# Combining a mixture of experts: weights built during the experts' stage, results kept by slot, row-tiled products in the combine

## The reference, cut to what matters

```python
cap = int(EXPERT_CAPACITY * T / E)                       # 2 * 256 / 8 = 64
scores = jnp.einsum('BTC,CE->BTE', x, gate_w)
probs = jax.nn.softmax(scores, axis=-1)
top_p, top_idx = jax.lax.top_k(jnp.transpose(probs, (0, 2, 1)), cap)
xin = jnp.take_along_axis(x[:, None, :, :], top_idx[..., None], axis=2)
h = jax.nn.gelu(jnp.einsum('BElC,ECH->BElH', xin, w1), approximate=False)
y = jnp.einsum('BElH,EHC->BElC', h, w2)
y = y * top_p[..., None]
out = jnp.zeros((B, T, C), x.dtype).at[b_idx, top_idx].add(y)
...
x = x + gb * out
```

## Time and profile before

| | us |
|---|---|
| median of 3 runs | 1366.04 (1364.01 to 1376.72) |
| the profiled execution | 1369.83 |
| its span, first to last instruction | 1368.0 |
| mean granted TensorE clock in the span | 0.882 of full |

### The profile page before, as it was taken

How to read it: one execution, slowest core, us unless ns; L and a number is a source line. 1 busy time by engine, 2 the same in 40 slices (tenths; PEclk the granted TensorE clock), 3 DMA queues, 4 the chain that set the end, 5 groups by cost and what they waited for, 6 DMA issues and landing times. The chain is left out here.

```text
span 1368.0 us, 23917 instructions
## 1 busy us (share of the span) xinstructions
PE 1073.3 (78%) x6664; PEld 818.5 (60%) x6665; DVE 870.2 (64%) x1675; ACT 693.1 (51%) x1535; POOL 637.9 (47%) x938
## 2 busy tenths in 40 slices
PE   1999966899787799889998889973463399999950
PEld 1577742344386588778888788862242267777640
DVE  2477647201187599999999999992466633433327
ACT  1455432343244688888888888860242233433320
POOL 2000002100021689999999999980000556666630
PEclk9898857999999799999999999995555599999985
DMA  6000000111100200000000000003210011111135
GB/s 194 1 1 1 1 1 0 34 43 33 44 0 22 64 13 13 12 12 12 23 12 12 12 12 16 19 1 129 71 31 23 6 35 43 42 42 42 41 75 167
DMA packets 48617, 46.23 MB, mean 34 GB/s; under 512 B 4857, under 2 KB 44482, under 8 KB 48210
## 3 DMA queue, kind: packets, MB, share of 16 engines
q1 hardware_dynamic: 39474, 28.71, 7.3%
q0 software_dynamic: 4608, 9.45, 2.5%
q10 hardware_dynamic: 4496, 7.60, 1.6%
HBM read 36.74 MB, written 9.01 MB: 33 GB/s over the span
## 5 line engine op out<-in xcount | busy, mean ns | idle before, releaser
L1220 DVE TENSOR_TENSOR_SCAN s_hs<-s_dA,bank 128x1024 f32<-128x1024 f32 x128 | 291.5, 2277 | 11.2 <-PE bank L1617 10.5
L1477 POOL TENSOR_SCALAR s_dbuT<-s_dtuT,s_BT 128x256 f32<-128x256 f32 x512 | 242.3, 503 | 11.3 <-POOL s_bc L1415 5.4
L1338 ACT ACTIVATE s_dA<-s_dt,aneg 128x255 f32<-128x255 f32 x512 | 211.8, 495 | 0.2
L1617 PE MATMUL bank<-const,s_dbuT 128*128 128x128 f32 x1024 | 136.3, 277 | 3.1 <-POOL s_dbuT L1477 3.1
L1231 DVE TENSOR_TENSOR s_hc<-s_hs,bank 128x1024 f32<-128x1024 f32 (+1 forms) x128 | 130.2, 1017 | 5.0 <-PE bank L1644 1.6
L2142 PE MATMUL bank<-w,x_xT 128*128 x288 | 127.2, 565 | 5.4 <-issue 3.9
L1635 PE MATMUL bank<-const,s_hc 128*128 128x128 f32 x832 | 114.3, 276 | 21.1 <-DVE s_hc L1231 21.1
L1617 PEld LDWEIGHTS bank<-const,s_dbuT 128*128 128x128 f32 x1024 | 116.8, 143 | 6.5 <-POOL s_dbuT L1477 4.0
L1635 PEld LDWEIGHTS bank<-const,s_hc 128*128 128x128 f32 x832 | 95.7, 142 | 24.9 <-DVE s_hc L1231 24.9
L2180 ACT ACTIVATE x_a<-bank 128x448 f32<-128x448 f32 x72 | 39.2, 545 | 140.2 <-PE bank L2142 140.2
L2102 POOL DMA_INDIRECT x_xg<-hf_rows,x_src x72 | 69.8, 969 | 72.3 <-DVE x_src L2200 42.4
(11 more groups left out here) (303 smaller groups left out, 2332.1 us busy)
## 6 DMA issues: line engine op xcount, KB each, us to landing
s_Crow<-C_rows SPq DMA_DIRECT2D x48, 128.0 KB, 2.9
w<-in_w SPq DMA_DIRECT2D x16, 256.0 KB, 3.0
o_yr<-y_rows SPq DMA_DIRECT2D x8, 512.0 KB, 3.9
w<-in_w ACTq DMA_DIRECT2D x1, 3584.0 KB, 13.2
x_res<-in_x SPq DMA_DIRECT2D x4, 512.0 KB
gate<-gates_d SPq DMA_DIRECT2D x2, 1024.0 KB, 5.8
s_gate<-gates_d SPq DMA_DIRECT2D x2, 1024.0 KB, 7.4
hf_rows<-r_rows SPq DMA_DIRECT2D x8, 256.0 KB, 2.2
```

Source lines behind the costliest of these rows:

```text
L1220: dve.tensor_tensor_scan(flat(hs[:, j % 2]), flat(dA[:, j % RING]), bDbu[j % 2], 0.0, ALU.mult, ALU.add).then_inc(S["scanned"], 1)
L1338: ins = act.activation(dA[:, j % RING, h, n, 1:], dt[:, k, h, 1:], ACT.Exp, scale=m.aneg[:, h, 2 * j + n:2 * j + n + 1])
L1477: ins = pool.tensor_scalar(dbuT[:, j % RING, c, n, :], dtuT[:, k, c, :], BT[:, k, c, 2 * j + n:2 * j + n + 1], 1.0, ALU.mult, ALU.mult)
L1617: mm = pe.transpose(out[:, h, n, c * P:(c + 1) * P], dbuT[:, j % RING, c, n, h * P:(h + 1) * P], ident)
```

## The change

In five places:

- **Constants.** One column more: C_SLOT holds 1 + (partition mod 64).
- **Attention and combine.** The making of `m.spread` moves from POOL's start in attention to POOL in the combine, for its memory is used in between.
- **Route.** ACT copies the turned probabilities out (`chance`), SP stores them to device memory (`m.prob_d`, 128 KB). DVE makes the slot list a second time in bfloat16 (`listed16`), and SP stores it too (`m.place_d`, 64 KB).
- **Experts.** After the weights of each expert, SP spreads rows of `m.place_d` and `m.prob_d` over partitions: for the pair of sequences with the expert's number, each sequence's row of 2,048 entries (8 experts x 256 tokens) goes to 64 partitions, first sequence to the lower and second to the upper half. DVE then makes all the weights of that pair with one instruction, `(place == slot) * prob`, into `m.pickT`. The second product has its operands swapped: `g` is the weights' side and `w2` the moving side, 16 products of 128 columns per half in place of 4 of 512. Its result has the slot in the partition.
- **Combine.** No one-hots, transposes or copies are left. For each pair, half of the tokens and expert, two products over 64 rows each, one on the lower and one on the upper half of the array, into two different banks; then DVE's two products with the gate and one add. The loop is written out; four pairs have banks of their own. The gate load stays at the head, but now only DVE's first product waits for it.

Memory is laid out anew (`m.pickT` shares memory with `m.xin`, `m.taps` with `m.yT`).

```diff
@@ route_phase
-            tick(dve.tensor_copy(left[:], ps[0][:, 0:L]))
-            settle()
+            dve.tensor_copy(left[:], ps[0][:, 0:L]).then_inc(s_copied, 1)
+            dve.wait_ge(s_copied, 1)
...
             dve.tensor_tensor(listed[:], place[:], taken[:], ALU.mult).then_inc(s_out, 1)
+            dve.tensor_tensor(listed16[:], place[:], taken[:], ALU.mult).then_inc(s_list16, 1)
...
+        @block.scalar
+        def _(act):
+            act.wait_ge(s_copied, 1)
+            act.activation(chance[:], ps[0][:, 0:L], ACT.Copy).then_inc(s_chance, 1)
+
+        @block.sync
+        def _(sp):
+            rows = lambda t: t.rearrange("b (e t) -> (b e) t", e=E0)
+            sp.wait_ge(s_chance, 1)
+            sp.dma_start(rows(m.prob_d), chance[:]).then_inc(s_kept, 16)
+            sp.wait_ge(s_list16, 1)
+            sp.dma_start(rows(m.place_d), listed16[:]).then_inc(s_kept, 16)
+            sp.wait_ge(s_kept, 32)
@@ expert_phase, sync (after the two weight loads of an expert)
+                    sp.wait_ge(chosen[k], r + 1)
+                    for j in range(2):
+                        row = bass.ds(4 * r + 2 * k + j, 1)
+                        part = slice(CAP * j, CAP * (j + 1))
+                        for dst, src in ((place[k], m.place_d), (prob[k], m.prob_d)):
+                            sp.dma_start(dst[part, :], src[row, :].rearrange("o n -> (o n)").partition_broadcast(CAP))\
+                              .then_inc(spread[k], 16)
@@ expert_phase, tensor
                         for h in range(HC0):
                             pe.wait_ge(gelued[h], 4 * r + 2 * k + a + 2)
-                            mm = pe.matmul(ps[4 + a][:, :], w2[:, k, h, :], g[:, a, h, :], start=(h == 0),
-                                           stop=(h == HC0 - 1))
+                        for j in range(N // P):
+                            for h in range(HC0):
+                                mm = pe.matmul(ps[4 + a][:, j * D:(j + 1) * D], g[:, a, h, j * P:(j + 1) * P],
+                                               w2[:, k, h, :], start=(h == 0), stop=(h == HC0 - 1))
                         mm.then_inc(result[k][a], 1)
@@ expert_phase, vector (after the two copies to m.yT)
+                    dve.wait_ge(spread[k], 64 * (r + 1))
+                    dve.scalar_tensor_tensor(m.pickT[:, bass.ds(2 * r + k, 1), :].rearrange("p o n -> p (o n)"), place[k],
+                                             m.const[:, C_SLOT:C_SLOT + 1], prob[k], ALU.is_equal, ALU.mult)\
+                       .then_inc(chosen[k], 1)
@@ combine_phase (all of its old body goes)
         @block.sync
         def _(sp):
             sp.dma_start(gate[:], gate_rows(m, GB0)).then_inc(s_gate, 16)
             sp.wait_ge(s_gate, 16)
 
+        @block.gpsimd
+        def _(pool):
+            pool.tensor_copy(m.spread[:], m.const[:, C_REP + NST:C_REP + 2 * NST].unsqueeze(2).broadcast_to(
+                [P, NST, P])).then_inc(s_spread, 1)
+            pool.wait_ge(s_spread, 1)
+            pool.memset(m.spread[32:64], 0.0).then_inc(s_spread, 1)
+            pool.wait_ge(s_spread, 2)
+
         @block.tensor
         def _(pe):
...
+            for p in range(PAIRS):
+                if p >= 4:
+                    pe.wait_ge(s_read, 2 * (p - 3))
+                for c in range(NCH):
+                    for e in range(E0):
+                        for k in range(2):
+                            rows = slice(CAP * k, CAP * (k + 1))
+                            t = e * L + c * P
+                            mm = pe.matmul(ps[2 * (p % 4) + k][:, c * D:(c + 1) * D], m.pickT[rows, p, t:t + P],
+                                           m.yT[rows, e, p * D:(p + 1) * D], start=(e == 0), stop=(e == E0 - 1))
+                mm.then_inc(s_out, 1)
+
+        @block.vector
+        def _(dve):
+            dve.wait_ge(s_gate, 16)
+            for p in range(PAIRS):
+                dve.wait_ge(s_out, p + 1)
+                if p >= 2:
+                    dve.wait_ge(s_sum, p - 1)
+                for k in range(2):
+                    dve.tensor_tensor(out[:, p % 2, 2 * k:2 * k + 2, :],
+                                      ps[2 * (p % 4) + k][:, 0:L].rearrange("p (c d) -> p c d", c=NCH),
+                                      gate[:, 2 * p + k:2 * p + k + 1, :].broadcast_to([P, NCH, D]), ALU.mult)\
+                       .then_inc(s_read, 1)
+                dve.wait_ge(s_read, 2 * p + 2)
+                xs = m.x_res[:, 2 * NCH * p:2 * NCH * (p + 1), :]
+                dve.tensor_tensor(xs, out[:, p % 2], xs, ALU.add).then_inc(s_sum, 1)
+            dve.wait_ge(s_sum, PAIRS)
@@ build, before gather_phase
+                    whole = sb("xin", [P, 5 * E0 * L + E0 * B * CAP])
+                    m.xin = whole[:, 5 * E0 * L:].rearrange("p (e n) -> p e n", e=E0)
+                    m.pickT = whole[:, 0:PAIRS * E0 * L].rearrange("p (r n) -> p r n", r=PAIRS)
```

More of the change, by code:

```diff
@@ L493, in _ @@
                     .then_inc(S["w_own"], 1)
[L494 to L498, removed]
             pool.wait_ge(S["w_prep"], 1)
             pool.tensor_scalar(m.aneg[:], m.aneg[:], -1.0, 1.0, ALU.mult, ALU.mult).then_inc(S["w_own"], 1)
-            pool.wait_ge(S["w_own"], NH + 4)
+            pool.wait_ge(S["w_own"], NH + 2)
             def body(n0, n1, n2, n3, n4, odd):
@@ L778, in route_phase @@
         listed = sb("listed", [P, L])
+        listed16 = sb("listed16", [P, L], BF16)
+        chance = sb("chance", [P, L])
         s_in, s_own, s_out, s_back = sem("rt_in"), sem("rt_own"), sem("rt_out"), sem("rt_back")
+        s_copied, s_chance, s_list16, s_kept = sem("rt_copied"), sem("rt_chance"), sem("rt_list16"), sem("rt_kept")
         ident = m.const[:, C_ID:C_ID + P]
@@ L894, in expert_phase @@
         g = sb("g", [P, 2, HC0, N])
+        place1 = sb("place1", [P, E0 * L], BF16)
+        place = [m.spread[:].rearrange("p n q -> p (n q)"), place1[:]]
+        prob = [m.xn2[:, TILES // 2 * k:TILES // 2 * (k + 1), :].rearrange("p t d -> p (t d)") for k in range(2)]
+        spread = [sem(f"e_spread{k}") for k in range(2)]
+        chosen = [sem(f"e_chosen{k}") for k in range(2)]
         loaded = [sem(f"e_loaded{k}") for k in range(2)]
@@ L903, in _ @@
         def _(pool):
-            for free in (*result[0], *result[1], *gelued, *kept):
+            for free in (*result[0], *result[1], *gelued, *kept, *chosen):
                 pool.sem_inc(free, 1)
@@ L972, in combine_phase @@
-        s_gate, s_out, s_sum = (sem("c_" + n) for n in ("gate", "out_ps", "sum"))
-        ident = m.const[:, C_ID:C_ID + P]
-        iota = m.const[:, C_IOTA:C_IOTA + CAP]
-        block = ctx.enter_context(nc.Block())
[L978 to L1015, removed]
-                        if b is not None:
-                            dve.wait_ge(S["pickT_ps"][k], a)
-                        lists(a, k)
-                if b is not None:
-                    for k in range(2):
-                        dve.wait_ge(s_out, 2 * b + k + 1)
-                        dve.wait_ge(s_sum, 2 * b + 2)
-                        dve.tensor_tensor(out[:, k], ps[6 + k][:, 0:L].rearrange("p (c d) -> p c d", c=NCH),
-                                          gate[:, bass.ds(2 * b + k, 1), :].broadcast_to([P, NCH, D]),
-                                          ALU.mult).then_inc(S["prod"][k], 1)
-                    for k in range(2):
-                        dve.wait_ge(S["prod"][k], b + 2)
-                        xs = m.x_res[:, bass.ds(b * 2 * NCH + k * NCH, NCH), :]
-                        dve.tensor_tensor(xs, out[:, k], xs, ALU.add).then_inc(s_sum, 1)
-            dve.wait_ge(s_gate, 16)
-            rounds(dve, body)
@@ L1034, in _ @@
+        gate = sb("gate2", [P, B, D])
+        out = sb("moe0", [P, 2, 2 * NCH, D])
+        s_gate, s_out, s_read, s_sum, s_spread = (sem("c_" + n) for n in ("gate", "out_ps", "read", "sum", "spread"))
+        block = ctx.enter_context(nc.Block())
         @block.sync
@@ L1069, in _ @@
-            rounds(pe, body)
-        @block.scalar
-        def _(act):
-            def body(a, b):
-                if a is not None:
-                    for k in range(2):
-                        act.wait_ge(S["pickT_ps"][k], a + 1)
-                        for q in range(2):
-                            act.activation(pickT[:, k, 2 * q:2 * q + 2, :],
-                                           ps[2 * k + q][:, :].rearrange("p (a t) -> p a t", a=2),
-                                           ACT.Copy).then_inc(S["pickT"][k], 1)
-                    for k in range(2):
-                        act.wait_ge(S["y_ps"][k], a + 1)
-                        act.activation(ysl[:, k], ps[4 + k][:, :].rearrange("p (a d) -> p a d", d=D), ACT.Copy)\
-                           .then_inc(S["ysl"][k], 1)
-            rounds(act, body)
+            for p in range(PAIRS):
[9 more added lines that the diff above has]
+                mm.then_inc(s_out, 1)
@@ L2332, in sb @@
```

(3 more changed lines are left out.)

42 lines of the change are left out of this document (5 added, 37 removed).

## The result

| | before | after |
|---|---|---|
| median (range), us | 1369.32 (1364.01 to 1376.72), 4 runs | 1332.05 (1331.23 to 1342.37), 4 runs |
| profiled execution, us | 1369.83 | 1332.48 |
| its span | 1368.0 | 1330.7 |
| ratio of the runs | | 0.9741, 95% interval 0.970 to 0.978 |

A forecast was written before the change was run, and what follows sets the result against it. PE alone was taken to bound the experts, PE and DVE in turn the combine. The combine stretch falls from 71.25 to 34.5 us (-36.75), costs add 6.2, together -30.5: 1336 us, range 1329 to 1350 (0.82).

The forecast's parts named there:

- Overlap of the halves: Combine: products on the two row halves run at once, 256 pairs of records at 0.114 us, 29.2 us.
- Clock at the combine's start: Combine: PE restarts at half speed for some 4.4 us, costing 2.2 us (0 to 3.4).
- The seam before the combine: Between last choice and PE's first combine record: barrier 1.2 us plus first latency 0.3 us.
- Swap of the operands: Experts' second product: 16 products of 128 columns replace 4 of 512 per half, +2.2 us.
- The last choice: End of experts: DVE's eighth choice follows the last copy with nothing beside it, +2.3 us (2.1 to 2.5).
- Route: Route's end: the block waits until the 64 KB listed16 store lands, taken as 2.4 us; +1.7 us (1.4 to 2.2).
- Start of the experts: PE's gap and clock return where the experts' stage begins: the forecast sum had no term for either.
- The gate load, the spreads, POOL's move: Combine, experts and attention: gate load covered by banks, spreads hidden behind PE, POOL otherwise idle; each priced at 0.
- No gain, the halves do not overlap: Rival, combine: 512 records take 58.4 us, kernel 1365 us, the same as before; chance 0.10.
- The clock stays at half: Rival, combine: a grant of 0.50 through it was listed as a wrong sign; size and chance not in the given text.
- The chance of a slower kernel: Experts: 0.04, laid on the spreads becoming the bound, each expert waiting for its 2.10 MB, about 1570 us.
- The 38 us by the ratio of 0.77: Combine: the skill's less favourable row-tile speedup would make 29.2 us into 38, the result 9 us later.

The follow-up runs named there:

- experiment 8: Kernel before and changed kernel, both unedited, each profiled a second time on another chip: spans 1390.5 us before and 1364.1 us after.
- experiment 6: Changed kernel with DVE's choice of an expert made ahead of the two result copies: 1337.7 us, 0.974 of the kernel before.
- experiment 1: Changed kernel with all 256 combine products reading rows 0 to 63 only: 1440.8 us, ratio 1.033 to the kernel before.
- experiment 2: Changed kernel with the half as outer and the expert as inner loop of the combine's products: 1412.8 us, ratio 1.014 to the kernel before.
- experiment 5: Changed kernel with each expert's four transfers over 64 partitions made two over 128, same bytes: 1336.9 us in one run.
- experiment 7: Experiment 6's kernel plus the first two experts' weights loaded during the gather stage: 1327.7 us, 0.9696 of the kernel before.

## Why the prediction was right

The predicted sum was -30.5 us. Up to the scan's start the first two profiles differ by 409.5 - 441.1 = -31.6, and the two of the other chip by -27.6. Ahead of the route stage, where the change was priced at 0, the profiles of after are 0.2 and 3.4 us longer (setup and attention). From route's first instruction on DVE to the scan's start the change is so -31.8 and -31.0 us. The medians of the first comparison are 37 us apart, and in its two profiles 5.7 of that lie in the later part, by chance as far as experiment 8 shows. The comparison in five rounds on one chip has 1365.3 - 1335.2 = 30.1 us.

- **Overlap of the halves: right.** 29.2 us were predicted at full clock. With the clock full throughout (experiment 6) it took 28.86, 0.056 a record.
- **Clock at the combine's start: right.** 2.2 us predicted; 30.18 - 28.86 = 1.3 in the first profile, 2.9 in each of two others (31.76 and 31.74 us).
- **The seam before the combine: a little too dear.** 1.2 + 0.3 us were put between the choice's end and PE's first record; it was 376.79 - 375.96 = 0.8.
- **Swap of the operands: right.** +2.2 predicted, 2.27 measured by undoing it.
- **The last choice: right.** +2.3 predicted, 2.35 measured; taking it away gave it back and the clock's loss too.
- **Route: mis-sized.** +1.7 was predicted from a landing of 2.4 us. The store landed in 1.6, and DVE's gap to the next stage went from 1.22 us to 1.88: **+0.7**:

```profile
219.63 1.49 DVE L833 TENSOR_TENSOR pick<-places,const 128x512 f32<-128x512 f32 x2 [1.88 <-PEq L104]
```

- **Start of the experts: missed.** PE's gap there grew from 5.82 to 6.45 us, because that stage's first transfer starts 1.3 us later, 0.5 more than the stages before account for; why is open. And the clock came back 6.0 us after PE's start instead of 3.3, which costs half the difference, 1.3. The sum had neither. The latter is one execution against another and not the change: the first 16 records took 8.77 us in the kernel before, but 9.93 when it was profiled again, 10.12 in the changed kernel and 8.52 with the same code in experiment 1. The four in this order:

```profile
256.07 8.77 PE L925 MATMUL bank<-xin,w 128*128 x16 [5.82 <-DMA w<-in_w]
```

```profile
254.92 9.93 PE L925 MATMUL bank<-xin,w 128*128 x16 [5.85 <-DMA w<-in_w]
```

```profile
257.51 10.12 PE L954 MATMUL bank<-xin,w 128*128 x16 [6.45 <-DMA w<-in_w]
```

```profile
259.28 8.52 PE L954 MATMUL bank<-xin,w 128*128 x16 [6.42 <-DMA w<-in_w]
```

PE's stretch in the stage was 115.26 us against 112.93 in the two second profiles, 2.33 more: the swap and nothing else.

- **The gate load, the spreads, POOL's move: right at 0.** The spreads' price was 7.7 to 13.5 us an expert; it was 8.5 to 9.2 (0.61 to 0.66 of 14 us) with the weights.

That the sum came so near is in part luck. Route, the seam and the clock at the combine's start were 1.0, 0.7 and 0.9 us too dear in the first profile, the products 0.3; the 0.6 of the gap and the 1.3 of clock at the experts' start were missing. And the low end of the range has a slip: 1333 less 3 is 1330, not 1329.

The two stores of the route stage (KB, us from issue to landing):

```profile
prob_d<-chance SPq DMA_DIRECT2D x1, 128.0 KB, 1.7
place_d<-listed SPq DMA_DIRECT2D x1, 64.0 KB, 1.6
```

Two rivals were priced wrongly, though they did not come true. "No gain, the halves do not overlap" was put at 58.4 us and no change; with one half at a time it was 108.5 us and a kernel 3.3% slower than before. "The clock stays at half" was treated as another, independent case; it was the same one. The chance of a slower kernel had thus been laid on the wrong mechanism. On the other side, the pair of rows in attention, eight records in two row tiles as fast as four in one, was the right evidence, and here it was enough; it came from blocks of four records a tile, and experiment 2 shows that blocks of 16 would not have done. The 38 us by the ratio of 0.77 of the Trainium skill ("TensorE: Matmul & The Clock Gate", section "Measured speedup vs the span model") is not what two halves with 128 columns showed: 57.3 us of serial steps (512 x 0.112) against 28.9 are 1.98 times. The rule of the Trainium skill on 64 partitions ("SBUF — State Buffer", section "Door 1: The DMA port swizzle") agrees with experiment 5 in direction: 237 GB/s against 328 over 128 partitions, weights included in both.

## What to carry to other kernels

Look first for work that exists only to change a layout: 192 of the old combine's 448 PE records, all of its ACT work and its POOL work were transposes and copies. Swapping the operands one stage earlier made those of the results needless for 2.3 us; building the weights in their final layout from spread rows made the others needless, for 2.3 us of the last choice and 0.7 in the route stage. When products use half of the rows, alternate the halves product by product; the order of two loops decided here between 30 and 88 us. And work that is "moved into idle time" should be checked at its last instance: the eighth choice stood on the path, and putting it ahead of the copies gave 3.6 us in the stages.

## What the runs showed of the hardware that was not expected

- A gapless stream of products on rows 0 to 63 alone was granted 0.50 of the clock for all of its 107 us; the same stream on all 128 rows was granted 1.00 after 6 us, and two interleaved halves after 2.8 to 6.1 us. PE's busy share was full in all three.
- Products of the other row half overtake within PE's queue, but only some way: with 16 records of one half at a time a step was 0.172 us at half clock, against 0.212 for a single half. At each change of half three records of the new half ran beside records of the old.
- Broadcasts to 64 partitions kept the DMA engines busy for 0.61 to 0.66 of a stretch of 14 us, the same bytes in half as many transfers to 128 partitions for 0.41 to 0.50.
- Executions differ by the clock that attention is granted: it was over by 199.4 us (mean grant 0.84), 205.9 (0.81) and 218.8 (0.75) in three profiles with the same code for it. The first of these, from the timing in experiment 7:

```profile
24.00:199.40 175.40, 149.26 (x1184) 110.40 (x1184) 106.76 (x393) 82.72 (x218) 7.53 (x12) 0.84 0.03 7
```

That spread of 19 us is over half of the change's effect, so a difference of a few microseconds has to be read from the stages.
